# Exponentials ahead of the low parts, the low part behind the shift, and the norms' Newton chain on GpSimd

## The chip, the cores and the metric

The kernel runs on one core of one Trainium2 chip. The metric is device time in microseconds (us) of that core. The time before is the median of three runs.

## The reference

Sixteen batches of 256 tokens with 256 features go through cross-attention and a mixture of experts; each has a layer norm ahead and a residual behind:

```python
x = x + xattn(layernorm(x), ctx, ...)     # 16 heads of 16, 77 keys per batch, softmax
x = x + moe(layernorm(x), ...)            # router 256 -> 8, softmax, top 2 of 8 experts
# expert: (silu(x @ gate) * (x @ up)) @ down, 256 -> 1024 -> 256, weighted and summed
layernorm(x) = (x - mean(x)) / sqrt(var(x) + 1e-5)
```

## The kernel before

The kernel has two stages. The first stage does the attention and the routing of all batches and writes each normalised token, with its routing weights, to the region of its experts in HBM. The second stage takes these rows in tiles of 128 through the experts; TensorE bounds it. All matmuls are made of fp16 high and low parts, three products each.

The first stage is a software pipeline with an order written out by hand for each engine. A **round** (`body(n, a, b, c, r, z)`) works on six batches at once, each one stage on: `n` is loaded, `a` is normalised and projected, `b` is in the middle of attention, `c` finishes attention and gets its residual, `r` is normalised again and routed, `z` is scattered to HBM. Eighteen rounds run, those from the seventh to the sixteenth in a hardware loop of two rounds each. A round has eight units `u` = 0 to 7; a unit is four heads of 128 tokens. Unit u goes through the engines like this:

- TensorE: `score(u)` (lines L564 to L566, output of 308 columns), `turn_probs(u)` (L633), `take_high(u)` (L640, subtracts the high part from the turned values in PSUM), `weigh_values(u)`. In step u of a round the order is score(u+2), weigh_values(u-2), take_high(u-1), turn_probs(u), then an extra part: u=1 turns x and the attention output (L581, L666), u=2 projects q, u=3 projects the output (L678 is its last part), u=4 turns the rows (L689), u=5 is the router, u=7 projects k and v.
- VectorE: `maximum(u+1)` (L1162), `shift(u+1)` (L1168, waits for turn_probs(u-1), whose input it overwrites), and for the one unit 7 `low_probs` (L1173). Extra parts are `inner` (between maximum and shift) and `outer` (after the shift).
- ScalarE: `low_probs(u-1)` for units 0 to 6 (L905, waits for take_high(u-1)), `exponentials(u+1)` (L872, waits for shift(u+1)), `split_probs(u)` (L878, the high part, waits for turn_probs(u)), then the extra part: u=0 norm of x (L913), u=1 split_x and split_att, u=2 norm of x2 (L913), u=3 split_q, u=4 copy_x2 (L889), u=7 router_exp (L900).
- GpSimd: in this order once per round `split_kv` (L1597 to L1609), `make_rows` (L1617, L1622, L1625), `split_cx` (L1588, L1590), and `scatter`, four indirect DMAs (L1642); the third waits until the first has landed. In rounds 2 to 4 it also splits the weights of the first expert (`split_expert`).

The layer norms of `n` and `c` share one **Newton chain** for 1/sqrt (`statistics`, VectorE, L1091 to L1120): four `bn_aggr`, then 13 dependent instructions on 4 elements per partition. It starts in u=4; `between()` puts one instruction of it after each other part of the round. ScalarE's norm of x at u=0 of the next round is the first to wait for it (semaphore `ln`).

Of the kernel before, what the change touches and what calls it, by code (L numbers as in the profile page):

```python
# [14 lines left out]
P = 128  # L15
# [34 lines left out]
RSQRT_SEED = 0x5F3759DF  # L50
LN_STEPS = 1 + 3 + 9 + 1
SHORT = 2
# [39 lines left out]
def build(nc, x, ctx_t, w_q, b_q, w_k, b_k, w_v, b_v, w_o, b_o, router_w, gate_w, up_w, down_w, out):  # L92
# [4 lines left out]
    with ExitStack() as stack:  # L97
# [43 lines left out]
        ln_var = sb("ln_var", [P, 2 * NT])  # L141
        ln_tmp = sb("ln_tmp", [P, 2 * NT])
        ln_rstd = sb("ln_rstd", [P, 2 * NT])
        ln_bias = sb("ln_bias", [P, 2 * NT])
# [133 lines left out]
        x2_summed = sem("x2_summed")  # L278
        ln = sem("ln")
        x2n_ready = sem("x2n_ready")  # L280
        x2_turned = sem("x2_turned")
# [94 lines left out]
        def early_pieces(n):  # L376
# [5 lines left out]
            return ()  # L382

        def is_first(j):

            return bool(j) and j.reg is None and j.plus == 0
# [23 lines left out]
        def of_act(u):  # L410

            return len([w for w in LOW_ON_ACT if w <= u])

        def pieces_at(e, j, s):
# [413 lines left out]
        def _(act):  # L828
# [87 lines left out]
            def body(n, a, b, c, r, z):  # L916
# [10 lines left out]
                         7: [(r, router_exp)]}  # L927
                for u in range(UNITS):
                    if (at := unit(c, b, a, u - 1)) and at[1] in LOW_ON_ACT:
                        low_probs(*at)  # L930
                    if at := unit(c, b, a, u + 1):
                        exponentials(*at)
                    if b:
                        split_probs(b, u)
                    for at, stage in extra.get(u, []):
                        if at:
                            stage(at)
# [84 lines left out]
        def _(dve):  # L1022
# [10 lines left out]
            def prepare():  # L1033
                dve.memset(ln_mv[:], 0.0).then_inc(bias_ready, 1)
                dve.memset(bo_parts[:], 0.0).then_inc(bo_ready, 1)
                dve.memset(row_ones[:], WS).then_inc(bo_ready, 1)
                dve.wait_ge(bias_ready, 1)

            def prepare_first(n0):
# [27 lines left out]

            def statistics(m, n, c):


                cols = slice(0 if n else NT, 2 * NT if c else NT)
                var, tmp, rstd, bias, mv = ln_var[:, cols], ln_tmp[:, cols], ln_rstd[:, cols], ln_bias[:, cols], ln_mv[:, cols, :]
                done = 0

                def step(ins):
                    nonlocal done
                    ins.then_inc(ln, 1)
                    done += 1

                def settle():  # L1080

                    after(dve, ln, m.value(LN_STEPS, done))


                if n:
                    after(dve, x_summed, n.value(1, 1))
                if c:
                    after(dve, x2_summed, c.value(1, 1))
                apart(dve, passed)
                for at in range(2 * NT)[cols]:  # L1090
                    ins = dve.bn_aggr(ln_mv[:, at, :], ln_stats[:, at, :])  # L1091

                step(ins)
                yield
                settle()
                step(dve.tensor_scalar(var, mv[:, :, 1], EPS, None, ALU.add))
                yield
                settle()
                step(dve.tensor_scalar(tmp.bitcast(I32), var.bitcast(I32), 1, None, ALU.logical_shift_right))
                yield  # L1100
                settle()

                if n:
                    after(dve, xn_ready, n.value(NT))
                if c:
                    after(dve, x2n_ready, c.value(NT))
                step(dve.tensor_scalar(rstd.bitcast(I32), tmp.bitcast(I32), -1.0, float(RSQRT_SEED), ALU.mult, ALU.add))
                for _ in range(3):
                    yield
                    settle()  # L1110
                    step(dve.tensor_tensor(tmp, rstd, rstd, ALU.mult))
                    yield
                    settle()
                    step(dve.scalar_tensor_tensor(tmp, tmp, -0.5, var, ALU.mult, ALU.mult))
                    yield
                    settle()
                    step(dve.scalar_tensor_tensor(rstd, tmp, 1.5, rstd, ALU.add, ALU.mult))
                yield
                settle()
                step(dve.scalar_tensor_tensor(bias, mv[:, :, 0], -1.0, rstd, ALU.mult, ALU.mult))  # L1120
                assert done == LN_STEPS

# [176 lines left out]
            def body(n, a, b, c, r, z):  # L1299
# [15 lines left out]
                if n and not b:  # L1315
# [7 lines left out]
                         3: [(n, lambda j: sum_x(j, 0, xin, x_in, 16, x_summed)),  # L1323
                             (r, lambda j: high_rows(j, rows_at(j)))],
                         4: [(c, residual)]}
                outer = {0: [(a, full_kv)],
                         1: [(c, lambda j: normalize(j, 1))],
                         2: [(c, low_att)],
                         4: [(c, lambda j: sum_x(j, 1, x2, x2_ready, 1, x2_summed)), (a, lambda j: low_q(j, j.plus % 2)),
                             (m, lambda j: start(statistics(j, n, c)))],  # L1330
                         5: [(b, lambda j: normalize(j, 0))],

# [4 lines left out]
                for u in range(UNITS):  # L1337
# [4 lines left out]
                    if following:  # L1342
                        maximum(*following)
                        between()
                    if (at := unit(c, b, a, u - 1)) and at[1] not in LOW_ON_ACT:
                        low_probs(*at)
                        between()
                    for at, stage in inner.get(u, []):
# [3 lines left out]
                    if following:  # L1352
                        shift(*following)
                        between()
                    for at, stage in outer.get(u, []):
# [7 lines left out]
            def filling(n, a):  # L1363

                if not a:
                    prepare()
                    sum_x(n, 0, xin, x_in, 16, x_summed)
                    for _ in statistics(n, n, None):
                        pass
                    prepare_first(n)  # L1370
                    return
                full_kv(a)
                sum_x(n, 0, xin, x_in, 16, x_summed)
                for k, _ in enumerate(statistics(n, n, None)):
                    if k == LN_STEPS // 2:
                        low_q(a, a.plus % 2)
                maximum(a, 0)
                shift(a, 0)
                prepare_later()
# [154 lines left out]
        def _(pool):  # L1534
# [15 lines left out]

            pool.memset(ones16[:], 1.0).then_inc(const_ready, 1)
            pool.iota(expert_i[:], pattern=[[1, E]], base=0, channel_multiplier=0).then_inc(const_ready, 1)
            pool.iota(region_i[:], pattern=[[REGION, E]], base=0, channel_multiplier=0).then_inc(const_ready, 1)
# [91 lines left out]
            def body(n, a, b, c, r, z):  # L1645
# [6 lines left out]
                if not a:  # L1652
                    if n:
                        write_pads()
                if z:
                    scatter(z, z.plus % 2, 2)
                if pieces := early_pieces(n):
# [60 lines left out]
```

## Time and profile before

| | us |
|---|---|
| median of three runs | 918.75 (918.18 to 919.05) |
| the profiled execution | 920.07 |
| its span in the trace | 918.1 |
| first stage, about | 0 to 341 |
| second stage alone, TensorE 98 to 100% busy | from 400 |

The profile page gives busy time per engine, waits and the chain that ended last. A wait is idle time of an engine just before an instruction, with the instruction that released it. Matmul records give the start well and the end by a model. In the first stage a round takes some 20 us.

### The profile page before, as it was taken

The page shows a single profiled execution, that of the slowest core. Times are in us where ns is not written, and L with a number is a line of the kernel's source. Part 1 is how long each engine was busy: PE and PEld are TensorE (multiplying, and loading weights), DVE is VectorE, ACT ScalarE, POOL GpSimd, SP SyncE. Part 2 cuts the span into 40 slices and gives each one's busy share as a digit, 9 for nine tenths or more (in the row PEclk, how much of TensorE's full clock was granted, in tenths as well). Part 3 has the DMA queues.
Part 4 walks back from the last instruction along what each step waited for, and adds up shares of the span by engine and source line. Part 5 has one row for each costly group of instructions (what it writes and reads, how often), then busy time and mean ns, then how long its engine had stood idle before and what let it go on. Part 6 is the DMA issues. An engine that isn't in the chain of part 4 may idle for free.

```text
span 918.1 us, 31885 instructions
## 1 busy us (share of the span) xinstructions
PE 850.5 (93%) x11936; PEld 774.2 (84%) x11936; DVE 600.2 (65%) x1932; ACT 478.9 (52%) x900; POOL 298.6 (33%) x427
## 2 busy tenths in 40 slices
PE   4898998989989889699999999999999999999995
PEld 3677777777777678589999999999999999999995
DVE  7779788878887766367466447546655647544542
ACT  5777777777777776245244325334434525332331
POOL 4789343434444334342221122222112222221122
PEclk9999899999999979899999999999999999999999
DMA  6212322222222342397256236324524732223221
GB/s 219 77 46 58 88 79 65 77 69 67 71 88 70 90 147 84 102 190 169 35 101 132 35 59 139 68 31 100 127 35 79 153 59 33 31 31 36 35 35 18
DMA packets 109875, 74.03 MB, mean 81 GB/s; under 512 B 66444, under 2 KB 99802, under 8 KB 109818
## 3 DMA queue, kind: packets, MB, share of 16 engines
q1 hardware_dynamic: 83898, 36.09, 16.3%
q0 software_dynamic: 13536, 19.85, 12.1%
q10 hardware_dynamic: 12384, 17.35, 7.6%
q8 instruction: 34, 0.56, 0.3%
q14 instruction: 23, 0.19, 0.1%
HBM read 36.27 MB, written 26.80 MB: 69 GB/s over the span
## 4 chain that ended last, share of the span: by engine, by line
PE 60%; issue 3%; DVE 3%; ACT 2%; DMA 1%; POOL 1%; ACTq 0%; DVEq 0%; POOLq 0%
PE bank L566 13%; PE bank L564 13%; PE bank L565 13%; PE bank L759 6%; PE bank L760 6%; PE bank L761 6%; PE bank L640 1%; DMA out<-y_sb,tok_row 1%; PE bank L633 1%; DVE e_lo L1296 1%; ACT pt_hi L878 1%; DVE h_full L1432 1%; ACT probs L872 0%; DMA expert_rows<-rows,slot_u 0%; DVE h_lo L1438 0%
## 5 line engine op out<-in xcount | busy, mean ns | idle before, releaser
L564 PE MATMUL bank<-xg,e_hi 128*128 128x128 f16 x2176 | 374.4, 220 | 2.7 <-issue 1.9
L565 PE MATMUL bank<-xg,e_hi 128*128 128x128 f16 x2176 | 374.3, 220 | 2.0 <-issue 2.0
L566 PE MATMUL bank<-xg,e_lo 128*128 128x128 f16 x2176 | 374.3, 220 | 1.7 <-issue 1.7
L1665 POOL DMA_INDIRECT out<-y_sb,tok_row x67 | 108.5, 1620 | 425.9 <-DVE y_sb L1427 404.2
L564 PEld LDWEIGHTS bank<-xg,e_hi 128*128 128x128 f16 x2176 | 213.9, 98 | 6.9 <-issue 3.5
L565 PEld LDWEIGHTS bank<-xg,e_hi 128*128 128x128 f16 x2176 | 213.9, 98 | 2.7 <-issue 1.2
L566 PEld LDWEIGHTS bank<-xg,e_lo 128*128 128x128 f16 x2176 | 213.9, 98 | 1.9 <-issue 1.9
L942 ACT ACTIVATE g_act<-bank 128x512 f32<-128x512 f32 x136 | 81.1, 596 | 225.4 <-PE bank L566 217.4
L1432 DVE SCALAR_TENSOR_TENSOR h_full<-bank,g_act 128x512 f32<-128x512 f32 x136 | 94.0, 691 | 122.1 <-ACT g_act L942 117.5
L759 PE MATMUL bank<-e_hi,h_hi 128*128 128x256 f16 x544 | 148.9, 274 | 4.9 <-DVE h_lo L1438 3.1
L760 PE MATMUL bank<-e_lo,h_hi 128*128 128x256 f16 x544 | 148.9, 274 | 0.0
L761 PE MATMUL bank<-e_hi,h_lo 128*128 128x256 f16 x544 | 148.9, 274 | 0.0
L947 ACT ACTIVATE h_hi<-h_full 128x512 f16<-128x512 f32 x136 | 85.6, 630 | 106.2 <-DVE h_full L1432 106.2
L1438 DVE TENSOR_TENSOR h_lo<-h_full,h_hi 128x512 f16<-128x512 f32 x136 | 94.4, 694 | 50.3 <-ACT h_hi L947 46.6
L905 ACT ACTIVATE pt_lo<-bank 77x512 f16<-77x512 f32 x112 | 66.2, 591 | 48.7 <-PE bank L640 46.5
L633 PE MATMUL bank<-ident,probs 128*77 128x128 f32 x512 | 81.0, 282 | 0.0
L1642 POOL DMA_INDIRECT expert_rows<-rows,slot_u x64 | 63.3, 990 | 46.0 <-issue 22.3
L878 ACT ACTIVATE pt_hi<-bank 77x512 f16<-77x512 f32 x128 | 74.2, 580 | 0.9 <-remote 0.5
L872 ACT ACTIVATE probs<-probs 128x308 f32<-128x308 f32 x128 | 58.1, 454 | 29.1 <-DVE probs L1168 28.2
L633 PEld LDWEIGHTS bank<-ident,probs 128*77 128x77 f32 x512 | 67.1, 152 | 6.6 <-issue 0.8
L759 PEld LDWEIGHTS bank<-e_hi,h_hi 128*128 128x128 f16 x544 | 53.4, 98 | 10.5 <-DVE h_lo L1438 4.3
L1162 DVE TENSOR_REDUCE row_max<-bank 128x4 f32<-128x308 f32 x128 | 59.9, 468 | 2.6 <-issue 1.6
(184 smaller groups left out, 1681.2 us busy)
## 6 DMA issues: line engine op xcount, KB each, us to landing
e_stage<-in_gate_w ACTq DMA_DIRECT2D x24, 256.0 KB
e_stage<-in_up_w ACTq DMA_DIRECT2D x22, 256.0 KB
e_stage<-in_down_w ACTq DMA_DIRECT2D x20, 256.0 KB
expert_rows<-pads SPq DMA_DIRECT2D x8, 530.0 KB
xin<-in_x SPq DMA_DIRECT2D x16, 256.0 KB, 2.9
xres<-in_x SPq DMA_DIRECT2D x16, 256.0 KB
out<-x SPq DMA_DIRECT2D x16, 256.0 KB
k_diag<-k_parts SPq DMA_DIRECT2D x124, 9.6 KB
```

Of the source, the lines that this page charges most:

```text
L564: pe.matmul(dst, a_hi(c), b_hi(c), start=c == 0, stop=False)
L565: pe.matmul(dst, a_hi(c), b_lo(c), start=False, stop=False)
L566: mm = pe.matmul(dst, a_lo(c), b_hi(c), start=False, stop=ends and c == chunks - 1)
L633: mm = pe.matmul(ps_probs[u % 2][0:KS, h * P:(h + 1) * P], probs[:, u % 2, h, :], ident[:], is_transpose=True, start=h == 0, stop=h == HG - 1)
L759: pe.matmul(ps_y[:, 0:D], h_hi[:, f, :], e_hi[:, parity, at:at + D], start=f == 0, stop=False)
L760: pe.matmul(ps_y[:, 0:D], h_hi[:, f, :], e_lo[:, parity, at:at + D], start=False, stop=False)
L761: mm = pe.matmul(ps_y[:, 0:D], h_lo[:, f, :], e_hi[:, parity, at:at + D], start=False, stop=f == FC - 1)
L878: act.activation(pt_hi[:, u % 2, :], ps_probs[u % 2][0:KS, :], ACT.Copy).then_inc(pt_hi_ready, 1)
L947: act.activation(h_hi[:, s * FS:(s + 1) * FS, :].rearrange("p f t -> p (f t)"), h_full[:, s, :], ACT.Copy).then_inc(h_hi_ready, 1)
L1432: dve.scalar_tensor_tensor(h_full[:, s, :], ps_up[s][:], H_DOWN, g_act[:, s, :], ALU.mult, ALU.mult).then_inc(h_ready, 1)
L1438: dve.tensor_tensor(h_lo[:, s * FS:(s + 1) * FS, :].rearrange("p f t -> p (f t)"), h_full[:, s, :], h_hi[:, s * FS:(s + 1) * FS, :].rearra ...
L1665: pool.indirect_dma_start(out, bass.IndirectOffsetOnAxis(tok_from[:], 0), y_from[:], None, compute_op=ALU.add).then_inc(added, 16)
```

## The change

It has four parts. (1) ScalarE does exponentials(u+1) ahead of low_probs(u-1). (2) VectorE does shift(u+1) ahead of low_probs(u-1), which concerns unit 7 alone, in step u=0. (3) VectorE's parts move: the residual of `c` goes from before the shift to after it in u=4, and its statistics (`bn_stats`) and the start of the chain go from u=4 to u=5, behind `normalize`. (4) The Newton chain is written anew with 12 instructions on VectorE or 16 on GpSimd (which gets constants from `ln_const` and no fused instruction). In rounds 5 to 17 GpSimd does it, between the second and the third of its scatters; VectorE keeps the four `bn_aggr` (`gather`). Elsewhere VectorE keeps it. The bias at the end of the chain is one fused instruction or two plain ones. In the diff the loop over `u` is ScalarE's, the tables `inner` and `outer` VectorE's, and the part from `m = n` on GpSimd's.

```diff
-LN_STEPS = 1 + 3 + 9 + 1
+LN_STEPS = 2 + 12 + 2
...
+        def by_pool(n, b):
+            return bool(b) and not early_pieces(n)
...
+        def newton(eng, m, n, c, fused):
...
+            after(eng, ln_gathered, m.value(1, 1))
+            settle()
+            apart(eng, passed)
+            step(eng.tensor_scalar(var, mv[:, :, 1], EPS, -0.5, ALU.add, ALU.mult))
+            yield
+            settle()
+            if n:
+                after(eng, xn_ready, n.value(NT))
+            if c:
+                after(eng, x2n_ready, c.value(NT))
+            apart(eng, passed)
+            step(eng.tensor_scalar(rstd.bitcast(I32), var.bitcast(I32), -0.5, float(RSQRT_SEED - (1 << 30) - (1 << 22)), ALU.mult, ALU.add))
+            for _ in range(3):
+                yield
+                settle()
+                step(eng.tensor_tensor(tmp, rstd, rstd, ALU.mult))
+                yield
+                settle()
+                step(eng.tensor_tensor(tmp, tmp, var, ALU.mult))
+                yield
+                settle()
+                if fused:
+                    step(eng.scalar_tensor_tensor(rstd, tmp, 1.5, rstd, ALU.add, ALU.mult), 2)
+                else:
+                    step(eng.tensor_tensor(tmp, tmp, ln_const[:, 0, cols], ALU.add))
+                    yield
+                    settle()
+                    step(eng.tensor_tensor(rstd, tmp, rstd, ALU.mult))
...
                 for u in range(UNITS):
+                    if at := unit(c, b, a, u + 1):
+                        exponentials(*at)
                     if (at := unit(c, b, a, u - 1)) and at[1] in LOW_ON_ACT:
                         low_probs(*at)
-                    if at := unit(c, b, a, u + 1):
-                        exponentials(*at)
...
-                             (r, lambda j: high_rows(j, rows_at(j)))],
-                         4: [(c, residual)]}
+                             (r, lambda j: high_rows(j, rows_at(j)))]}
...
-                         4: [(c, lambda j: sum_x(j, 1, x2, x2_ready, 1, x2_summed)), (a, lambda j: low_q(j, j.plus % 2)),
-                             (m, lambda j: start(statistics(j, n, c)))],
-                         5: [(b, lambda j: normalize(j, 0))],
+                         4: [(c, residual), (a, lambda j: low_q(j, j.plus % 2))],
+                         5: [(b, lambda j: normalize(j, 0)), (c, lambda j: sum_x(j, 1, x2, x2_ready, 1, x2_summed)),
+                             (m, lambda j: gather(j, n, c) if by_pool(n, b) else start(statistics(j, n, c)))],
...
-                    if (at := unit(c, b, a, u - 1)) and at[1] not in LOW_ON_ACT:
-                        low_probs(*at)
-                        between()
...
                     if following:
                         shift(*following)
                         between()
+                    if (at := unit(c, b, a, u - 1)) and at[1] not in LOW_ON_ACT:
+                        low_probs(*at)
+                        between()
...
+                m = n or (c and c + 3)
                 if z:
-                    scatter(z, z.plus % 2, 2)
+                    scatter(z, z.plus % 2, 2, range(NT))
+                if m and by_pool(n, b):
+                    for _ in newton(pool, m, n, c, False):
+                        pass
+                if z:
+                    scatter(z, z.plus % 2, 2, range(NT, 2 * NT))
```

## Rows read from the trace of the kernel before

**Rows 1.** Busy time by stretch: length, then busy us of each engine, clock, DMA.

```profile
180.00:240.00 60.00, 54.55 (x694) 45.22 (x691) 48.83 (x203) 46.23 (x97) 25.17 (x48) 0.97 0.25 74
...
400.00:500.00 100.00, 99.63 (x1494) 95.63 (x1492) 62.96 (x149) 44.00 (x74) 25.50 (x19) 1.00 0.62 127
```

**Rows 2.** Waits of 60 to 340 us: total, times, longest.

```profile
ACT pt_lo L905 <- PE bank L640: 39.4, 49, 2.8
ACT probs L872 <- DVE probs L1168: 22.3, 40, 2.0
...
PEld bank L564 <- DVE probs L1168: 12.4, 20, 0.9
...
DVE x L1197 <- PE bank L678: 11.1, 13, 1.1
```

**Rows 3.** Timeline of ScalarE over one round: start, us, line, tiles, idle before.

```profile
219.73 0.21 ACT L900 ACTIVATE expl<-expl 128x16 f32<-128x16 f32 x1
220.97 0.46 ACT L872 ACTIVATE probs<-probs 128x308 f32<-128x308 f32 x1 [1.03 <-DVE probs L1168]
...
221.81 1.08 ACT L913 ACTIVATE xn<-xin,ln_bias,ln_rstd 128x256 f32<-128x256 f32 x2
...
227.91 0.59 ACT L905 ACTIVATE pt_lo<-bank 77x512 f16<-77x512 f32 x1
228.87 0.46 ACT L872 ACTIVATE probs<-probs 128x308 f32<-128x308 f32 x1 [0.36 <-DVE probs L1168]
229.23 0.57 ACT L878 ACTIVATE pt_hi<-bank 77x512 f16<-77x512 f32 x1
...
238.73 0.59 ACT L905 ACTIVATE pt_lo<-bank 77x512 f16<-77x512 f32 x1 [1.94 <-PE bank L640]
...
240.05 0.21 ACT L900 ACTIVATE expl<-expl 128x16 f32<-128x16 f32 x1
```

**Rows 4.** Timeline of VectorE over the same round.

```profile
219.87 0.69 DVE L1173 TENSOR_TENSOR pt_lo<-bank,pt_hi 77x512 f16<-77x512 f32 x1 [1.15 <-ACT pt_hi L878]
220.47 0.46 DVE L1168 TENSOR_TENSOR probs<-bank,row_max 128x308 f32<-128x308 f32 x1
...
230.12 0.69 DVE L1197 SCALAR_TENSOR_TENSOR x<-bank,xres 128x512 f32<-128x512 f32 x1 [0.91 <-PE bank L678]
230.73 0.47 DVE L1168 TENSOR_TENSOR probs<-bank,row_max 128x308 f32<-128x308 f32 x1
...
233.32 0.48 DVE L1168 TENSOR_TENSOR probs<-bank,row_max 128x308 f32<-128x308 f32 x1
```

**Rows 5.** Timeline of TensorE over the same round.

```profile
219.41 0.66 PE L633 MATMUL bank<-ident,probs 128*77 128x128 f32 x4
...
236.84 0.41 PE L640 MATMUL bank<-pt_hi,minus 77*77 77x512 f16 x1 [0.37 <-issue]
```

**Rows 6.** Timeline of GpSimd over the same round.

```profile
221.94 0.31 POOL L1597 CAST k_parts<-k_full 128x154 f16<-128x154 f32 x1 [4.15 <-DVE v_full L1142]
222.33 0.47 POOL L1600 TENSOR_TENSOR k_parts<-k_full,k_parts 128x154 f16<-128x154 f32 x1
...
233.46 0.97 POOL L1642 DMA_INDIRECT expert_rows<-rows,slot_u  x1 [0.30 <-issue]
235.81 0.97 POOL L1642 DMA_INDIRECT expert_rows<-rows,slot_u  x1 [1.38 <-DMA expert_rows<-rows,slot_u]
237.08 0.97 POOL L1642 DMA_INDIRECT expert_rows<-rows,slot_u  x1 [0.30 <-issue]
```

**Rows 7.** Groups of 120 to 300 us, shapes apart: busy us, mean ns.

```profile
L1111 DVE TENSOR_TENSOR ln_tmp<-ln_rstd 128x4 f32<-128x4 f32 x27 | 4.3, 158 | 0.3
...
L1617 POOL COPY rows<-token_i 128x2 int32<-128x2 int32 x9 | 1.6, 181 | 0.0
```

**Rows 8.** The query on line L1254: duration min, median, max.

```profile
L1254 DVE TENSOR_TENSOR weight<-both,prob_inv x16: 165/174/554, 79.8 to 365.0; 128x16 f32<-128x16 f16 x16
```

**Rows 9.** Timeline of SyncE's DMA issues over the same round.

```profile
224.29 5.10 SPq L363 DMA_DIRECT2D k_diag<-k_parts  x8
```

More of the change, by code:

```diff
@@ L142, in build @@
         ln_tmp = sb("ln_tmp", [P, 2 * NT])
+        ln_const = sb("ln_const", [P, 2, 2 * NT])
         ln_rstd = sb("ln_rstd", [P, 2 * NT])
@@ L279, in build @@
         ln = sem("ln")
+        ln_gathered = sem("ln_gathered")
+        ln_set = sem("ln_set")
         x2n_ready = sem("x2n_ready")
@@ L412, in of_act, with ln_cols, step, settle @@
             return len([w for w in LOW_ON_ACT if w <= u])
+        def ln_cols(n, c):
+            return slice(0 if n else NT, 2 * NT if c else NT)
+        def newton(eng, m, n, c, fused):
+            cols = ln_cols(n, c)
+            var, tmp, rstd, bias, mv = ln_var[:, cols], ln_tmp[:, cols], ln_rstd[:, cols], ln_bias[:, cols], ln_mv[:, cols, :]
+            done = 0
+            def step(ins, of=1):
+                nonlocal done
+                ins.then_inc(ln, of)
+                done += of
+            def settle():
+                after(eng, ln, m.value(LN_STEPS, done))
+            after(eng, ln_gathered, m.value(1, 1))
[26 more added lines that the diff above has]
+                    step(eng.tensor_tensor(rstd, tmp, rstd, ALU.mult))
+            yield
+            settle()
+            if fused:
+                step(eng.scalar_tensor_tensor(bias, mv[:, :, 0], -1.0, rstd, ALU.mult, ALU.mult), 2)
+            else:
+                step(eng.tensor_tensor(tmp, mv[:, :, 0], rstd, ALU.mult))
+                yield
+                settle()
+                step(eng.tensor_tensor(bias, tmp, ln_const[:, 1, cols], ALU.mult))
+            assert done == LN_STEPS
         def pieces_at(e, j, s):
@@ L1037, in prepare @@
                 dve.wait_ge(bias_ready, 1)
+                dve.wait_ge(ln_set, 2)
             def prepare_first(n0):
@@ L1066, in sum_x, with gather @@
                 ins.then_inc(ready, 1)
[L1068 to L1082, printed above, removed]
+            def gather(m, n, c):
                 if n:
@@ L1088, in statistics @@
                     after(dve, x2_summed, c.value(1, 1))
+                after(dve, ln, m.value(LN_STEPS))
                 apart(dve, passed)
-                for at in range(2 * NT)[cols]:
+                for at in range(2 * NT)[ln_cols(n, c)]:
                     ins = dve.bn_aggr(ln_mv[:, at, :], ln_stats[:, at, :])
-                step(ins)
+                ins.then_inc(ln_gathered, 1)
+            def statistics(m, n, c):
+                gather(m, n, c)
                 yield
[L1095 to L1121, printed above, removed]
+                yield from newton(dve, m, n, c, True)
             def low_x(j):
@@ L1374, in filling @@
                 for k, _ in enumerate(statistics(n, n, None)):
-                    if k == LN_STEPS // 2:
+                    if k == 7:
                         low_q(a, a.plus % 2)
@@ L1551, in _ @@
             pool.memset(ones16[:], 1.0).then_inc(const_ready, 1)
+            pool.memset(ln_const[:, 0], 1.5).then_inc(ln_set, 1)
+            pool.memset(ln_const[:, 1], -1.0).then_inc(ln_set, 1)
             pool.iota(expert_i[:], pattern=[[1, E]], base=0, channel_multiplier=0).then_inc(const_ready, 1)
```

## The prediction

> **What bounds the kernel now.** I read the stretches first [rows 1]. From 400 us TensorE is busy 99.6 of 100 us, and the change touches nothing there. In the first stage it is busy 54.6 of 60 us, VectorE 48.8, ScalarE 46.2 and GpSimd 25.2: no engine is full, and four engines hand units to each other. So what a change is worth is read from the waits [rows 2]. ScalarE waits 39.4 us for TensorE's take_high (L640) and 22.3 us for VectorE's shift (L1168); TensorE's weight loads wait 12.4 us for the shift; VectorE waits 11.1 us for the output projection (L678). Then I read one round as timelines, from 219.73 us, where router_exp (L900) ends a round, to 240.05 us: 20.32 us [rows 3]. I call its start T. Three places are late in it:
>
> - u=0. low_probs(7) on VectorE starts at 219.87, shift(1) behind it at 220.47 [rows 4]. exponentials(1) waits 1.03 us for that, and norm x starts at 221.81 [rows 3]. shift(1) needs nothing of low_probs(7).
> - u=4. The residual waits 0.91 us and starts at 230.12; shift(5) is behind it at 230.73, and shift(6) comes at 233.32 [rows 4].
> - u=7. low_probs(6) on ScalarE starts at 238.73 after 1.94 us of idle time [rows 3], 1.89 us after the start of take_high(6) at 236.84, which takes some 0.41 [rows 5]. The profile names no cause for the other 1.4 us. It lies over the fourth scatter (237.08 to 238.05 [rows 6]).
>
> **The change part by part.** I follow one round with the new orders and the old durations; the sums are against the profiled execution, 920.07 us (span 918.1), 1.3 us above the median of 918.75. I use them as differences.
>
> *shift(1) first, at u=0.* shift(1) can run before 219.4, in VectorE's idle 1.15 us ahead of low_probs(7) [rows 4]. exponentials(1) follows L900 at 219.86, split_probs(0) waits for turn_probs(0) to end at 219.41 + 0.66 = 220.07 [rows 5], so it starts at 220.2 and norm x at 220.7 instead of 221.81: 1.1 us earlier. But VectorE still has low_probs(7) at 219.87; behind it k, v, maximum, shift(2) and normalize(1) only lose the 0.39 us of the moved shift and a short wait, so they come 0.5 us earlier. By the projection of q the gain is the smaller of the two, 0.55 us.
>
> *Exponentials ahead of low_probs.* This costs where the shift is late: low_probs(2) ran at 227.91 in the hole before exponentials(4) at 228.87 [rows 3], which waited 0.36 us for the shift. Now it comes behind it and pushes split_probs(3) back by its 0.49 us. exponentials(4) comes some 0.3 us earlier, so split_probs(3) starts at 229.45 instead of 229.23, a loss of 0.2 us. TensorE, which was busy with the output projection, starts turn_x2 still 0.3 us early. It gains at u=7: exponentials(8), 0.35 us, is done in the wait for take_high(6).
>
> *Residual behind the shift, statistics at u=5.* shift(5) goes from 230.73 to about 229.0, the residual to 229.4, low_q then waits for split_q until 230.7, and shift(6) goes from 233.32 to about 231.9. exponentials(6) then waits for ScalarE's own queue, and comes 1.0 us earlier. With the other units the lead is 0.55 us on TensorE at u=7 (take_high(6) at 236.3). No one waits for x2 early but its store and the statistics, which now end at 233.95.
>
> *The chain leaves VectorE.* 13 instructions of 158 ns [rows 7], some 0.1 us apart when interleaved, 1.5 us in all. They lay where VectorE then idled, so I cost their removal at 0; the cover is the wait for split_probs(7).
>
> So a round is shorter by 0.55 us at take_high(6), plus 0.35 for exponentials(8): 0.9 us if the unexplained 1.4 us stays. If it goes with the scatter, ScalarE is free at 237.7 (2.3 us early), but TensorE is not: behind take_high(6) come turn_probs(7), k and v (1.1 us), score(10), weigh_values(6) and turn_probs(0), which starts at 238.8, 19.4 us after the last one at 219.41. VectorE then has full_kv early, which gives another 0.5 us in the next round: 1.4 us. I take 1.1 us, between 0.9 and 1.4, as the stall seems tied to a scatter that moves but may come back at the new place.
>
> *The chain on GpSimd.* 16 dependent instructions. The trace has no such instruction; the nearest are a copy of two elements, 181 ns [rows 7], and the gap between dependent ones, 221.94 + 0.31 to 222.33 = 0.08 us [rows 6]. With two inputs I take 0.20, so 16 x 0.28 = 4.5, plus 0.5 for the extra waits of the first two (a further wait costs up to 0.3, as between two scatters [rows 6]): 5.0 us. Bounds: 16 x 0.26 = 4.2 us from below. From above a two-input instruction of 128x154 takes 0.47 [rows 6], so 16 x 0.55 + 0.5 = 9.3 us; 4 elements are much nearer to the copy. The chain starts behind the second scatter (ends at 234.43 [rows 6], about 234.1 in the new round) at 234.4 = T + 14.7 and ends at T + 19.7. Norm x wants it at T' + 1.0, where T' is the next T. So the round can't be shorter than 14.7 + 5.0 - 1.0 = 18.7 us. My round is 20.3 - 1.1 = 19.2: hidden, with 0.5 us to spare. If the chain takes more than 6.6 us, the round is longer than the old one.
>
> VectorE can hold GpSimd up, and be held: one instruction (L1254) takes 165 ns mostly and 554 at the longest [rows 8], in a round where it overlapped GpSimd's v_parts. One such block is 0.4 us, within the spare. "SBUF — State Buffer" of the Trainium skill (Who interferes with whom) states that a VectorE instruction with two SBUF inputs contends with a GpSimd one that reads SBUF, and the row agrees.
>
> *What is queued behind it on GpSimd.* Scatters 3 and 4 (from 235.81 [rows 6]) come at T + 20.0 and T + 21.3, end at T' + 3.1, and split_kv, at T + 2.2 now, starts at T' + 3.2 and ends k's part at T' + 4.1. SyncE issues the eight spreads of k from T + 4.6 for 5.1 us [rows 9], so they are hardly moved; score(8) needs them at T + 13.6. The rows of the next batch wait for the landing of scatter 4, some 2 us, at T' + 5.1, where GpSimd now idles until 228.6 = T + 8.9. Cost 0.
>
> *Ends.* Thirteen rounds (5 to 17) have all four parts: 13 x 1.1 = 14.3 us. Rounds 1 to 4 have only the orders, and the chain on VectorE starts 1.2 us later; I cost them at 0 (0 to -2). After round 17 the norm of the last but one batch starts at once and waits for GpSimd's chain, 0.5 us. The second stage keeps its length. Sum: -14.3 + 0.5 = -13.8 us, so 920.07 goes to 906.3 and the median to 905.
>
> **The rivals.**
>
> *GpSimd's chain sets the round and makes it longer* (slower, 0.15). Place: norm x at u=0. It decides from 6.6 us, 0.38 per step. For it: two-input work on GpSimd is slower per element than on VectorE and every step waits for the last; against it: the copy of 181 ns. At 0.40 per step, about the middle between the 0.26 and 0.55 of the bounds, 16 x 0.40 + 0.5 = 6.9, round 20.6, 13 x 0.3 = +4, and the later scatters come on top: 921 to 928. "GPSIMD Engine Reference" of the Trainium skill (Performance versus the Vector engine) speaks against the change: elementwise work with two inputs takes about twice VectorE's time. By it a step is 2 x 0.158 + 0.08 = 0.40 us, this same case; the row of the small copy bears it out only by 181 to 158.
>
> *The orders cancel* (same or a small gain). exponentials first costs 0.2 to 0.5 us in units where the shift is late, and if this happens in more units than u=3 it eats the 0.9. Round 19.8 to 20.3: 912 to 919. Chance 0.22, of which 0.07 within 0.2%.
>
> *The stall at u=7 goes and the leads add up.* Round down to GpSimd's bound of 18.7: 13 x 1.6 = 21 us, 898; 893 to 899. Chance 0.11.
>
> **How the numbers follow.** Forecast (899 to 912, likeliest 905): 0.52. The bigger gain 0.11, the small gain 0.15, no change 0.07, slower 0.15. 0.2% of 918.75 is 1.8 us, about what a measurement of this kernel can tell from no change. Faster 0.78, same 0.07, slower 0.15. The range 897 to 919 leaves out most of the slower case and the end of the bigger gain, 0.2 together.
>
> **What would show it.** exponentials(1) without the 1.03 us behind VectorE; shift(5) ahead of the residual; the time between the L900s 18.7 to 19.5 us; 16 small instructions on GpSimd in 4.5 to 5.5 us, over before norm x could start. I am wrong if norm x shows idle time released by GpSimd, if ScalarE's waits for the shift only move from L872 to L905, or if TensorE starts waiting for k_diag.

## The result, and the profile after

The change made the kernel slower: 928.8 us (median of 4 runs, 925.6 to 936.4) against 918.5 us for the kernel before in the same session (4 runs), a ratio of 1.0127 with a 95% interval of 1.0088 to 1.0165. A second session gave 932.1 us and 1.0167 [1.0091, 1.0242]. The forecast was 905, with a range of 897 to 919. The profiled execution took 931.52 us with a span of 929.6, 11.5 us more than the span of before.

The page of the kernel after, part 1 (engine, busy us, share of the span, instructions):

```profile
span 929.6 us, 32045 instructions
PE 859.4 (92%) x11936; PEld 773.8 (83%) x11936; DVE 590.6 (64%) x1757; ACT 478.9 (52%) x900; POOL 341.7 (37%) x637
```

The waits of the kernel after over the first stage, 60 to 345 us, whose counterpart is [rows 2]:

```profile
ACT probs L938 <- DVE probs L1198: 42.3, 44, 2.6
...
PEld bank L630 <- ACT pt_lo L971: 19.2, 42, 1.4
ACT pt_hi L944 <- PE bank L699: 18.4, 17, 3.0
...
DVE inv_sum L1209 <- remote: 10.6, 6, 2.1
...
POOL ln_var L443 <- DVE ln_mv L1144: 10.2, 4, 2.8
...
ACT pt_lo L971 <- PE bank L706: 7.6, 23, 0.8
```

ScalarE's largest wait, for take_high (L706, was L640), fell from 39.4 to 7.6 us, with the 1.94 us at the end of the round. Its wait for VectorE's shift (L1198, was L1168) rose from 22.3 to 42.3 us, TensorE's weight loads waited 19.2 us for low_probs (5.6 before), and waits appeared that were not there. So the stall was removed and its time was paid elsewhere. One round at full clock shows where. ScalarE in the kernel after:

```profile
255.63 0.59 ACT L944 ACTIVATE pt_hi<-bank 77x512 f16<-77x512 f32 x1 [1.17 <-PE bank L699]
256.12 1.08 ACT L979 ACTIVATE xn<-xin,ln_bias,ln_rstd 128x256 f32<-128x256 f32 x2
...
258.72 0.59 ACT L944 ACTIVATE pt_hi<-bank 77x512 f16<-77x512 f32 x1 [0.69 <-remote]
...
261.01 0.46 ACT L938 ACTIVATE probs<-probs 128x308 f32<-128x308 f32 x1 [0.73 <-DVE probs L1198]
261.38 0.57 ACT L971 ACTIVATE pt_lo<-bank 77x512 f16<-77x512 f32 x1
261.86 0.58 ACT L944 ACTIVATE pt_hi<-bank 77x512 f16<-77x512 f32 x1
...
264.45 0.46 ACT L938 ACTIVATE probs<-probs 128x308 f32<-128x308 f32 x1 [1.03 <-DVE probs L1198]
264.82 0.57 ACT L971 ACTIVATE pt_lo<-bank 77x512 f16<-77x512 f32 x1
265.30 0.58 ACT L944 ACTIVATE pt_hi<-bank 77x512 f16<-77x512 f32 x1
...
273.54 0.58 ACT L944 ACTIVATE pt_hi<-bank 77x512 f16<-77x512 f32 x1
274.01 0.21 ACT L966 ACTIVATE expl<-expl 128x16 f32<-128x16 f32 x1
...
276.31 1.08 ACT L979 ACTIVATE xn<-xin,ln_bias,ln_rstd 128x256 f32<-128x256 f32 x2
```

Take norm x as zero, and read when split_probs(u) (L878 before, L944 after) starts. Before, norm x is at 221.81 and the next one at 242.13; after, at 256.12 and 276.31.

| split_probs of unit | 1 | 2 | 3 | 4 | 5 | 6 | 7 | next norm x |
|---|---|---|---|---|---|---|---|---|
| before, us after norm x | 1.81 | 4.45 | 7.42 | 9.84 | 12.39 | 14.40 | 17.76 | 20.32 |
| after | 2.60 | 5.74 | 9.18 | 11.19 | 13.47 | 15.84 | 17.42 | 20.19 |
| lag | 0.79 | 1.29 | 1.76 | 1.35 | 1.08 | 1.44 | -0.34 | -0.13 |

1.78 us is won at unit 7, where the stall was. 0.79 is lost at unit 1 and 0.97 at units 2 and 3. The loss at unit 1 is mostly the 0.69 us above. It isn't TensorE's turn_probs(1), which was over at 257.12; it lies behind a scatter that GpSimd now issues there (257.17 to 258.14). TensorE's turn_probs(0) and turn_probs(1) in that round:

```profile
254.95 0.64 PE L699 MATMUL bank<-ident,probs 128*77 128x128 f32 x4
...
256.52 0.60 PE L699 MATMUL bank<-ident,probs 128*77 128x128 f32 x4
```

The losses at units 2 and 3 come with the 0.73 and 1.03 us in which exponentials wait for a shift, with low_probs (L971) and split_probs queued behind them. One round later the same scatters look like this. GpSimd in the kernel after:

```profile
268.88 0.97 POOL L1673 DMA_INDIRECT expert_rows<-rows,slot_u  x1 [0.30 <-issue]
270.43 0.19 POOL L443 TENSOR_SCALAR ln_var<-ln_mv 128x4 f32<-128x4 f32 x1 [0.58 <-issue]
270.97 0.20 POOL L452 TENSOR_SCALAR ln_rstd<-ln_var 128x4 int32<-128x4 int32 x1 [0.34 <-POOL ln_var L443]
271.25 0.20 POOL L456 TENSOR_TENSOR ln_tmp<-ln_rstd 128x4 f32<-128x4 f32 x1
271.52 0.20 POOL L459 TENSOR_TENSOR ln_tmp<-ln_tmp,ln_var 128x4 f32<-128x4 f32 x1
...
274.89 0.20 POOL L477 TENSOR_TENSOR ln_bias<-ln_tmp,ln_const 128x4 f32<-128x4 f32 x1
275.89 1.03 POOL L1673 DMA_INDIRECT expert_rows<-rows,slot_u  x1 [0.80 <-issue]
277.23 0.98 POOL L1673 DMA_INDIRECT expert_rows<-rows,slot_u  x1 [0.30 <-issue]
```

ScalarE and, in its own view, VectorE in that stretch:

```profile
278.75 0.59 ACT L971 ACTIVATE pt_lo<-bank 77x512 f16<-77x512 f32 x1 [1.01 <-remote]
```

```profile
278.72 0.26 DVE L1209 RECIPROCAL inv_sum<-bank 128x16 f32<-128x16 f32 x1 [2.08 <-remote]
```

Both engines start again within 0.03 us of each other, 0.5 us after the last scatter ended at 278.21. Before, low_probs(6) at 238.73 stood in the same relation to the fourth scatter (end 238.05, [rows 3, 6]). "remote" means that the profile found no event in the trace to name.

A round at full clock is thus about as long as before, not 1.1 us shorter. The 11.5 us have two sources. Norm x starts for the fifth time at 82.2 us, before at 78.5: 3.7 us lost in the early rounds. From its sixth to its sixteenth start it takes 213.1 us, before 203.0: 10.1 us more, with three rounds of 23.0 to 23.9 us by L966. (Between them 0.5 us and after them 1.7 us are won back.) The busy time of those stretches in the kernel after (length, busy us of PE, PEld, DVE, ACT and POOL, clock, DMA share, GB/s):

```profile
186.00:210.00 24.00, 20.26 (x236) 16.24 (x234) 16.39 (x58) 16.18 (x35) 12.14 (x34) 0.84 0.22 62
210.00:231.00 21.00, 20.00 (x244) 15.91 (x242) 16.45 (x57) 15.34 (x35) 11.29 (x30) 0.94 0.23 71
276.00:296.00 20.00, 17.53 (x229) 14.27 (x228) 15.37 (x55) 15.28 (x33) 11.63 (x32) 1.00 0.25 74
```

The long rounds are those in which the granted clock fell to its lower level of 1.2 GHz for a few us: from 100 to 300 us its mean was 0.98 before, 0.94 here and 0.97 in the repeat. The repeat of the same kernel had one such round (24.1 us) and ended at 929.0 us all the same: there the fifth start came at 82.7, the ten rounds took 206.9 us, and 2.5 us were lost behind the sixteenth start.

### The profile page after: what moved, and what is told of

Read it like the earlier page. It is cut to its first block, busy times and chain, and to the rows that moved or that the text cites. A ratio compares the mean times of both kernels' runs of the same rounds, so it can differ in the third digit from the quotient of the medians.

```text
span 929.6 us, 32045 instructions
## 1 busy us (share of the span) xinstructions
PE 859.4 (92%) x11936; PEld 773.8 (83%) x11936; DVE 590.6 (64%) x1757; ACT 478.9 (52%) x900; POOL 341.7 (37%) x637
## 4 chain that ended last, share of the span: by engine, by line
PE 57%; DVE 2%; issue 2%; ACT 1%; DMA 1%; POOL 1%; ACTq 0%; SPq 0%; another core or an unknown queue 0%; DVEq 0%; POOLq 0%
PE bank L632 13%; PE bank L630 13%; PE bank L631 12%; PE bank L825 6%; PE bank L826 6%; PE bank L827 6%; DMA raw_tail<-expert_rows 1%; DMA expert_rows<-rows,slot_u 1%; PE bank L699 1%; DVE e_lo L1326 0%; DVE h_full L1461 0%; POOL expert_rows L1673 0%; POOL rows L1653 0%; ACT pt_lo L971 0%; DVE probs L1198 0%
## 5 line engine op out<-in xcount | busy, mean ns | idle before, releaser
L944 ACT ACTIVATE pt_hi<-bank 77x512 f16<-77x512 f32 x128 | 75.2, 587 | 22.7 <-PE bank L699 19.1
L971 ACT ACTIVATE pt_lo<-bank 77x512 f16<-77x512 f32 x112 | 65.6, 586 | 14.0 <-PE bank L706 9.7
L630 PEld LDWEIGHTS bank<-v_parts,pt_hi 77*128 77x128 f16 x512 | 43.2, 97 | 31.4 <-ACT pt_lo L971 23.2
L1198 DVE TENSOR_TENSOR probs<-bank,row_max 128x308 f32<-128x308 f32 x128 | 60.7, 474 | 11.9 <-PE bank L699 9.5
```

The source lines that it names most:

```text
L630: pe.matmul(dst, a_hi(c), b_hi(c), start=c == 0, stop=False)
```

## The experiments

A is ScalarE's exponentials first, B VectorE's shift ahead of low_probs(7), C the move of residual and statistics, D the chain on GpSimd between the scatters. All ratios are to the kernel before on the same chip, with 95% intervals; below 1 is faster. The edits are shown shortened.

### Each order by itself

exp_first_only is the kernel before with A:

```diff
 for u in range(UNITS):
+    exponentials(u + 1)
     low_probs(u - 1)
-    exponentials(u + 1)
```

> The kernel before with ScalarE's new order alone. Scatter theory: within 0.5% of before, 914 to 923 us, since the scatters stay where they were. Order theory: 925 to 932 us, as all of the loss comes with it.

Measured 1.0036 [1.0003, 1.0069], 920.5 us, as the scatter theory had it.

shift_first_only is the kernel before with B:

```diff
-    low_probs(7)          # VectorE, u = 0
     shift(1)
+    low_probs(7)
```

> The kernel before with the shift ahead of low_probs(7) alone. Both theories: the wait of 1.03 us at u=0 goes, a gain of 0.3 to 0.6 us per round, 909 to 914 us. If it gains nothing, the 1.03 us was not on the path.

Measured 0.9931 [0.9903, 0.9959], 914.2 us, with most rounds of 19.6 to 19.9 us. This order is a gain of 6 us; A is a loss of 3.

residual_and_shift is B and C:

```diff
-4: residual, shift(5), sum_x(c), low_q, start(statistics)
+4: shift(5), residual, low_q
-5: normalize(b)
+5: normalize(b), sum_x(c), start(statistics)
```

> The kernel before with the shift ahead of low_probs(7) and VectorE's moves in u=4 and u=5, chain on VectorE, ScalarE in its old order. Theory of two costs (exponentials first makes low_probs and split_probs wait for a late shift; the chain on GpSimd moves the scatters onto u=0 and u=1): neither is in here, so 908 to 914 us. If the moved residual costs something of its own: 914 to 920 us.

Measured 0.9950 [0.9931, 0.9969], 913.6 us. The rounds from the sixth on are shorter than with B alone (197.8 against 199.5 us from the sixth to the sixteenth norm x), but the fifth norm x starts 2.5 us later than before (81.0).

### The change with one part taken back

chain_back_on_vector is A, B and C, without D:

```diff
-if m and by_pool(n, b):
-    for _ in newton(pool, m, n, c, False): pass
```

> All of the change but the chain on GpSimd: VectorE does the chain in every round, and the four scatters stand together again. Scatter theory (ScalarE and VectorE are held up when a scatter lies over the place where they wait for TensorE, and the chain pushed scatters 3 and 4 onto u=0 and u=1 of the next round, where this is on the path): 903 to 912 us, the idle time ahead of split_probs(0) gone, the wait of 1.4 us back at u=7. Order theory (exponentials ahead of low_probs is what costs): still 922 to 930 us, with the waits of exponentials(3) and (4) for the shift as after the change.

Measured 1.0026 [0.9998, 1.0054], 921.4 us: far from the scatter theory's 903 to 912 and just below the order theory's range. Its trace has the signs of both. low_probs(6) waits 0.8 to 1.4 us again in most rounds, and exponentials(3) and (4) wait 0.73 and 1.04 us for the shift. So the GpSimd chain isn't the whole loss, and A on top of B and C costs 7.6 thousandths (here VectorE's chain is the rewritten one of 12 instructions).

low_first_again is B, C and D, without A:

```diff
-    exponentials(u + 1)
     low_probs(u - 1)
+    exponentials(u + 1)
```

> The change with ScalarE's old order, low_probs(u-1) ahead of exponentials(u+1). Scatter theory: little better than the change, 922 to 928 us. Order theory: at or below the kernel before, 905 to 918 us.

Measured 0.9984 [0.9961, 1.0008], 916.0 us, in the order theory's range. Taking A back gives 1.4 to 1.8% of the time, far more than A alone costs.

after_again is the change once more, beside these:

> The change itself once more, for more runs of it beside the others: 925 to 932 us by both theories. In the low stretches of the clock the profile should show three or more of 4 to 8 us between 100 and 300 us, as its first profile did.

Measured 1.0167 [1.0091, 1.0242], 932.1 us. The sign of the clock missed: between 100 and 300 us its profile has one low stretch, at 271 us, and the end of one that began at 97, not three.

shift_and_chain is B and D, with the gather at u=4:

```diff
-4: sum_x(c), low_q, start(statistics)
+4: sum_x(c), low_q, gather (the chain follows on GpSimd)
```

> The kernel before with the shift first and the chain on GpSimd, but residual, statistics and gather in u=4 as before, and ScalarE in its old order. Theory that the scatters' new place costs: worse than the shift alone (914.2), 916 to 922 us. Theory that only exponentials first costs: 908 to 914 us.

Measured 1.0042 [1.0019, 1.0065]: D turns B's gain of 0.7% into a loss.

### The place of the scatters, with no chain in it

Two kernels keep the chain on VectorE and put 16 instructions of 4 elements, on a tile that no one reads, between GpSimd's second and third scatter. shift_first_late_scatters does so on B, orders_late_scatters on A, B and C:

```diff
-scatter(z, z.plus % 2, 2)
+scatter(z, z.plus % 2, 2, range(NT))
+for k in range(16):
+    after(pool, idled, z.value(16, k + 1))
+    pool.tensor_tensor(idle_tile, idle_tile, idle_tile, ALU.mult).then_inc(idled, 1)
+scatter(z, z.plus % 2, 2, range(NT, 2 * NT))
```

> The shift first alone, with 16 dependent idle instructions on a tile of its own between GpSimd's second and third scatter; the real chain stays on VectorE. So only the scatters move. Scatter theory: the wait of ScalarE's low_probs(6) at u=7 goes, and waits that end 0.6 to 0.8 us behind the third or fourth scatter come up at u=0 and u=1; the time rises above the shift alone (914.2) to 916 to 922 us. If the place of the scatters does not matter: 912 to 916 us.

> All orders of the change (exponentials first, shift first, VectorE's moves), the chain on VectorE, and 16 idle instructions between GpSimd's second and third scatter, so that only the scatters have the place of the change. If exponentials first and the scatters' place are what costs, alone and together: near the change, 925 to 932 us. If the chain on GpSimd costs something else (norm x waiting for it, VectorE held up): 919 to 925 us.

Measured 0.9992 [0.9972, 1.0012] on B, where nothing was added but the idle instructions and the later scatters: they take back B's gain, 0.6%, almost whole. The stall moves with the scatters: low_probs(6) waits 0.50 to 0.97 us (1.1 to 2.1 with B alone), and low_probs(0) now waits up to 1.13 us and starts 0.7 us after the end of a scatter. GpSimd and ScalarE:

```profile
203.06 0.96 POOL L1645 DMA_INDIRECT expert_rows<-rows,slot_u  x1 [0.30 <-issue]
```

```profile
204.72 0.59 ACT L907 ACTIVATE pt_lo<-bank 77x512 f16<-77x512 f32 x1 [1.13 <-remote]
```

On A, B and C: 1.0019 [0.9992, 1.0045], no more than without them (1.0026), and in the range that was expected if something else of the chain costs. The rows suggest why the place is nearly free there. With A, B and C alone split_probs(1) already starts some 2.2 us after norm x (1.8 before), as exponentials(2) wait some 0.3 us for the shift, so most of what the scatters delay was late anyway. So the place has a price, but with A it isn't where the rest of the loss comes from.

idle_after_gather starts those 16 instructions only when VectorE has gathered, as the real chain does:

```diff
+after(pool, ln, m.value(LN_STEPS, 1))
 for k in range(16):
```

> The three changes of order, the chain on VectorE, and 16 idle GpSimd instructions between scatters 2 and 3 that start only once VectorE has gathered the statistics, as the real chain does. Theory that the later place of scatters 3 and 4 (about 1 us later than with ungated idle instructions) is what the real chain costs: 927 to 933, with ScalarE or VectorE held at u=0 and u=1 behind those scatters. Rival, that the cost comes with the removal of the chain from VectorE or with the norm that it feeds: 920 to 924, as without the gate.

Measured 1.0047 [1.0019, 1.0075], 924.8 us, between the two; the interval overlaps that without the gate. In most rounds the last scatter ends 24.2 to 24.4 us after L900, against 23.6 to 23.8 without the gate and 24.3 to 25.2 in the change at full clock.

one_newton_round is the change with a short chain:

```diff
-for _ in range(3):
+for _ in range(3 if fused else 1):
```

> The whole change, with one Newton pass in place of three on GpSimd (it leaves out the accuracy that the other two passes give to the norm): 8 fewer instructions, so scatters 3 and 4 come 2.2 us earlier. Theory of the scatters' place: a large part of the 7 to 10 us that the real chain adds to the orders comes back, 918 to 924. Rival, that the chain costs by being fed from another engine at all: 927 to 933.

Measured 1.0053 [1.0028, 1.0077], 923.9 us. The last scatter mostly ends at 22.3 to 22.6 us, and 0.7 to 1.1% of the time comes back from 8 instructions fewer on an engine that is busy 37% of the time. The price of the chain depends on its length, though norm x doesn't wait for it. What is left of the price shows in the rows. TensorE, GpSimd and ScalarE of this kernel:

```profile
204.44 0.64 PE L700 MATMUL bank<-ident,probs 128*77 128x128 f32 x4
```

```profile
204.47 0.97 POOL L1674 DMA_INDIRECT expert_rows<-rows,slot_u  x1 [0.30 <-issue]
```

```profile
206.12 0.59 ACT L945 ACTIVATE pt_hi<-bank 77x512 f16<-77x512 f32 x1 [2.17 <-PE bank L700]
```

turn_probs(0) is over at 205.08, but split_probs(0) starts at 206.12, 0.68 us after the end of the last scatter (205.44), and norm x is right behind it. In nine of ten middle rounds it starts 0.67 to 0.82 us after a scatter's end. The scatters that come earlier than in the change thus meet the wait of u=0 instead of that of u=1: it isn't the latest scatter that costs most, but the one that lies over a wait.

scatters_before_chain is the change with the order on GpSimd turned round, all four scatters and then the chain:

```diff
 if z:
-    scatter(z, z.plus % 2, 2, range(NT))
+    scatter(z, z.plus % 2, 2)
 newton(pool, m, n, c, False)
-if z:
-    scatter(z, z.plus % 2, 2, range(NT, 2 * NT))
```

> The change with all four scatters ahead of GpSimd's chain. Scatter theory: the held-up waits of u=0 and u=1 go and the one at u=7 comes back, but the chain ends some 2.5 us later and norm x begins to wait for it by 1 to 2 us: 920 to 930 us, with idle time ahead of norm x released by GpSimd. If the scatters' place were no cause: above the change, over 932 us.

Measured 1.0315 [1.0265, 1.0364]. Now the chain is late for the norm. The query on its line L979 (idle time of its engine before it, by what ended it):

```profile
  POOL ln_bias L477: 17.7, 9
```

Nine waits of 17.7 us in all (1.0 to 3.5 us each, eight of them ahead of norm x), about the 15 to 19 us by which this kernel (947.4 us) is above the change. The time lies where it was expected if the scatters' place were no cause. But norm x waited longer than the 1 to 2 us that the other range stood on, and low_probs(6) waits up to 1.22 us again, so the time doesn't decide between the two. Behind the chain the scatters collide with the next round, and ahead of it they make the norm late.

### The early rounds

GpSimd splits expert weights in rounds 2 to 4, and C makes VectorE's chain run late in the round. The kernel after, VectorE and then ScalarE:

```profile
57.95 0.59 DVE L456 TENSOR_TENSOR ln_tmp<-ln_rstd 128x4 f32<-128x4 f32 x1 [0.17 <-DVE ln_rstd L463]
58.58 0.59 DVE L459 TENSOR_TENSOR ln_tmp<-ln_tmp,ln_var 128x4 f32<-128x4 f32 x1
...
59.64 0.16 DVE L472 SCALAR_TENSOR_TENSOR ln_bias<-ln_mv,ln_rstd 128x4 f32<-128x4 f32 x1
59.72 0.47 DVE L1192 TENSOR_REDUCE row_max<-bank 128x4 f32<-128x308 f32 x1
60.22 0.48 DVE L1198 TENSOR_TENSOR probs<-bank,row_max 128x308 f32<-128x308 f32 x1
```

```profile
60.73 0.46 ACT L938 ACTIVATE probs<-probs 128x308 f32<-128x308 f32 x1 [2.60 <-DVE probs L1198]
```

Steps that take 0.16 us elsewhere take up to 0.59, the next maximum and shift come behind them, and ScalarE waits 2.60 us. moved_from_round_5 is B, with C only from the fifth round on:

```diff
+moved = b and not early_pieces(n)
+old, new = (None, c) if moved else (c, None)
```

> Shift first and VectorE's moves, the latter only in rounds that split no expert weights (5 on), ScalarE's old order, chain on VectorE. The early rounds lost 2.5 us with the moves, as the chain then runs at the round's end while GpSimd splits weights; without that 909 to 912 us. If the early loss comes from elsewhere: as with the moves in all rounds, 913 to 914 us.

Measured 0.9903 [0.9871, 0.9934], 911.7 us; the fifth norm x starts at 79.2.

change_from_round_5 and low_first_from_round_5 make the same edit in the change and in the change without A:

> The whole change, with residual, second sum and gather moved only in the rounds that split no expert weights. Theory that the early rounds lose 2 to 3.5 us: 925 to 929, and the norm of x starts for the fifth time at about 79.5 instead of 82. Rival, that the early loss is made up later: 929 to 933.

> The change without the exponentials first, and with residual, second sum and gather moved only in the rounds that split no expert weights. If the early rounds' loss and the exponentials' order add up with the rest: 912 to 915. If the chain on GpSimd costs anything by itself, 915 to 919, well above the 911.7 of the same kernel with the chain on VectorE.

Measured 1.0074 [1.0036, 1.0113] and 0.9982 [0.9959, 1.0006]. In the change it gives back 5 to 9 thousandths (each ratio is known to some 4), and the fifth norm x starts at 78.6. The sixth start tells the same: 103.9 in the change, 101.5 with this edit, 100.7 before. Without A it gives nothing measurable, and the kernel stays 0.8% above moved_from_round_5, which differs from it only in D. So D costs by itself.

### The spacing of the scatters

moved_close_scatters is moved_from_round_5 with scatters that wait for no landing; moved_spaced_scatters lets each wait for the one before it:

```diff
-scatter(z, z.plus % 2, 2)
+scatter(z, z.plus % 2, 0)     # close
+scatter(z, z.plus % 2, 1)     # spaced
```

> As the one with the moves from round 5, and GpSimd issues the third and fourth scatter at once behind the second, without waiting for the landing of the first. They end 1.0 to 1.1 us earlier, so the held-up wait at u=7 (which ends 0.6 to 0.8 us behind the fourth scatter) shrinks: a gain of 0.3 to 1.0 us per round, 899 to 909 us. If that wait has nothing to do with the scatters: 909 to 912 us.

> Shift first, residual and statistics moved from the fifth round on, and each scatter also waits for the one before it to land. If an engine's wait is held only while scatters write descriptors back to back, wider gaps let waits end between them, but the last scatter ends later, towards u=0: 910 to 916. If the later end decides, 916 to 922.

Close: 1.0424 [1.0376, 1.0472], the opposite of what was expected. Its GpSimd, ScalarE, VectorE and TensorE, each from its timeline:

```profile
209.59 0.98 POOL L1646 DMA_INDIRECT expert_rows<-rows,slot_u  x1 [0.30 <-issue]
210.87 0.98 POOL L1646 DMA_INDIRECT expert_rows<-rows,slot_u  x1 [0.31 <-issue]
```

```profile
213.02 0.59 ACT L905 ACTIVATE pt_lo<-bank 77x512 f16<-77x512 f32 x1 [3.72 <-remote]
```

```profile
212.86 0.48 DVE L1162 TENSOR_REDUCE row_max<-bank 128x4 f32<-128x308 f32 x1 [2.12 <-remote]
```

```profile
209.35 0.41 PE L640 MATMUL bank<-pt_hi,minus 77*77 77x512 f16 x1 [0.16 <-issue]
213.67 0.20 PE L564 MATMUL bank<-v_parts,pt_hi 77*128 77x17 f16 x1 [2.79 <-ACT pt_lo L905]
```

take_high, on which low_probs waits, starts at 209.35 and takes 0.41 us. ScalarE goes on at 213.02, 1.2 us after the last of four scatters in a row; from round to round this wait is 2.6 to 4.0 us. TensorE idles 2.79 us for it, from 210.88 to 213.67, and the clock falls before that idle time is over. The windows of the same kernel:

```profile
212.00:214.00 2.00, 0.33 (x12) 0.34 (x12) 1.14 (x7) 0.98 (x3) 0.00 (x0) 0.71 0.18 68
214.00:216.00 2.00, 1.66 (x15) 1.34 (x13) 1.86 (x16) 1.26 (x3) 0.00 (x0) 0.50 0.00 0
```

Spaced: 0.9927 [0.9904, 0.9949]. GpSimd and ScalarE near the end of one of its rounds:

```profile
227.26 1.04 POOL L1646 DMA_INDIRECT expert_rows<-rows,slot_u  x1 [0.56 <-issue]
231.00 0.97 POOL L1646 DMA_INDIRECT expert_rows<-rows,slot_u  x1 [2.70 <-DMA expert_rows<-rows,slot_u]
234.29 0.97 POOL L1646 DMA_INDIRECT expert_rows<-rows,slot_u  x1 [2.32 <-DMA expert_rows<-rows,slot_u]
```

```profile
230.28 0.59 ACT L905 ACTIVATE pt_lo<-bank 77x512 f16<-77x512 f32 x1 [0.50 <-PE bank L640]
...
232.34 0.59 ACT L905 ACTIVATE pt_lo<-bank 77x512 f16<-77x512 f32 x1 [0.64 <-PE bank L640]
```

The wait of low_probs(6), 1.94 us before [rows 3] and 1.1 to 2.1 in moved_from_round_5, is 0.64 us here and 0.5 to 0.95 in the other rounds (the 0.50 is low_probs(5)'s), though the last scatter ends 5.1 us into the next round (at 238.80, L900 at 233.66). Two rounds take 38.8 to 39.3 us, those of moved_from_round_5 39.6 to 40.1. But the last rounds, where GpSimd waited up to 4.66 us for a landing, lost 6 us. spaced_while_loading keeps pairs there:

```diff
-scatter(z, z.plus % 2, 2)
+scatter(z, z.plus % 2, 1 if n else 2)
```

> Shift first, residual and statistics moved from the fifth round on, each scatter waits for the one before it to land, but only in rounds that still prepare a new batch; the last ones keep pairs. The spaced scatters gave rounds of 19.1 to 20.1 instead of 19.4 to 20.7, and lost about 6 us again in the last rounds, where a landing took 3.7 to 4.7 us. If that loss was the spacing's, 906 to 910, with rounds of 39 us for two. If it was not, 911 to 914.

Measured 0.9876 [0.9841, 0.9911], 909.1 us (905.7 to 910.0), as expected. This version is faster than the kernel before and the kernel after. That it is faster than moved_from_round_5 the ratios don't show, as their intervals overlap; the profiled executions took 193.4 and 197.1 us from the sixth to the sixteenth norm x.

## Why the prediction was wrong

**What held.** The stall at u=7 went, and shift(1) first gave its time: from the start of turn_probs(0) to norm x took 2.40 us before (219.41 to 221.81) and 1.17 after (254.95 to 256.12), where I had counted 1.1 less. Alone (B) it makes the kernel 0.7% faster. The GpSimd chain was forecast at 5.0 us and took 4.66 (270.43 to 275.09), 0.20 + 0.08 us per dependent step as estimated. The estimate of 0.40 us per step came from "GPSIMD Engine Reference" of the Trainium skill (Performance versus the Vector engine), which measured its ratio of two at 2048 elements; at 4 elements the trace disagrees. The rival that the chain sets the round by its length fails too: norm x never waited for GpSimd. The norm of x2 waited once, 0.69 us at 354.31, behind round 17 as forecast (0.5).

**The step that failed** is *What is queued behind it on GpSimd*, "Cost 0". I moved two scatters from u=6 and 7 to u=0 and 1 and looked only at who needs their data. What they cost is while they run: ScalarE and VectorE, waiting for TensorE's results, often go on only after them. Later scatters alone cost 3.9 us on the kernel with B (914.2 to 918.1). They also came later than forecast: the last one ended 4.2 us into the next round (278.21, L966 at 274.01), not 3.1. I had seen the stall lie over the fourth scatter and had written that it "may come back at the new place", but gave that 0.3 us per round in a range of 0.9 to 1.4; it came back with 0.8 (the table, unit 1). This isn't all of what the GpSimd chain costs, as said below.

**Exponentials first** was mis-sized. I found one late shift, at u=3, and charged 0.2 us net. The clean round has three, 0.73, 1.03 and 0.93 us (the third at 271.12), and each holds low_probs and split_probs back, on which TensorE waits. Measured: +0.4% alone, +0.8% on B and C, +1.4 to 1.8% on B, C and D. Why it grows with the other parts wasn't isolated. The rival *The orders cancel* had named this, more late units than u=3; its round of 19.8 to 20.3 us is the clean round of the kernel after (20.19). What it lacked are the early rounds and those at the lower clock. The gain at u=7 for exponentials(8) was real but went into the same 1.78 us.

**The early rounds**, costed at 0 to -2 us, cost 3.7 us by the fifth norm x, and 5 to 9 thousandths of the total in the change. VectorE's steps were slowed while GpSimd split weights. By "SBUF — State Buffer" of the Trainium skill (Who interferes with whom) a VectorE instruction with two inputs in SBUF contends with GpSimd reading there; the two steps of 0.59 us lie beside such an instruction and agree, but the step at 59.64 has two inputs, runs beside another instruction of GpSimd that reads SBUF, and kept 0.16. I had weighed that rule for the later rounds only.

**Sizes.** In ten middle rounds I expected -11 us (10 x 1.1) and the two profiled executions gave +10.1 and +3.9, the difference being how many rounds had the lower clock. The early rounds are the next 4 us. From the sixth to the sixteenth norm x one execution of each kernel took: before 203.0 us, A 202.0, B 199.5, B and C 197.8, A, B and C 201.9, B, C and D 201.2, all four 213.1 and 206.9.

**What stays open.** The parts don't add up. D costs 1.1% on B, 0.3% on B and C (0.8% with C from round 5) and 1.0 to 1.4% on A, B and C. Idle instructions in the chain's place cost 0.6% on B and nothing on A, B and C; started like the chain, 0.2% on top of A, B and C, which is within the noise. So on top of A most of what the real chain costs isn't the scatters' place as the idle instructions test it. The short chain leaves only 0.3%, and its rows explain that by a hold at u=0. The rest may be a scatter that ends up to 0.8 us later than with the idle instructions, a wait of GpSimd for VectorE, or how often the clock falls; the runs don't settle it. How a scatter holds the other engines' waits up is not seen in the trace either. That it does is shown by the spacing, which alone made the longest wait at the end of the round 2.6 to 4.0 us or 0.5 to 0.95, and by the idle instructions, which moved it.

## What to carry to other kernels

Before moving an instruction on a side engine, cost every DMA that it pushes along by what runs beside the DMA's issue, not only by who needs its data; a stall for which the profile names no cause, and that lies over such an issue, is the first suspect. In an in-order queue, putting the work that waits ahead of work that is ready is only right if it is never late: count it in every unit, not in the one where it was noticed. And test a reordering in the rounds that carry extra work too, since the same order gained in the late rounds and lost in the early ones.

## What the runs showed of the hardware

- While GpSimd issued indirect DMAs (0.97 us each), ScalarE's and VectorE's waits on TensorE's results often ended 0.5 to 0.9 us after the end of a pair of them: in the kernel before at 238.73 for an end at 238.05, in the kernel after together, at 278.72 and 278.75, for an end at 278.21. With four in a row ScalarE stood for 3.72 us and went on 1.2 us after the last; with each scatter behind the landing of the one before, it stood for 0.50 and 0.64 us in the round shown. Not every wait was held: in the kernel before low_probs started at 116.19, right behind take_high's end at 116.16, while a scatter ran (115.82 to 116.78).
- In the kernel with four scatters in a row the granted clock was 0.50, the level of 1.2 GHz, from 213.0 us on, in an idle time of TensorE from 210.88 to 213.67; it had been 1.00 until 212.0. In the kernel after the round with a mean clock of 0.84 took 23.9 us, that from 254 us at 1.00 took 20.1.
- GpSimd needed 0.20 us for an instruction with two inputs of 4 elements per partition, with 0.08 us between dependent ones; VectorE needed 0.16 us, and up to 0.59 while GpSimd split weights.
